# First attention of a two-layer kernel: scores with the keys as weights, the row maxima carried as two extra rows of the contraction

## What is computed

```
qh = layernorm_per_head((layernorm(x) @ Wq.T + bq))  * 16 ** -0.5      # 16 heads of 16
kh = layernorm_per_head(ctx @ Wk.T + bk);  vh = ctx @ Wv.T + bv
attn = softmax(einsum('bhqd,bhkd->bhqk', qh, kh), axis=-1)
x1 = x + einsum('bhqk,bhkd->bhqd', attn, vh).reshape(...) @ Wp.T + bp
router_logits = layernorm(x1) @ moe_router      # top 2 of 8 experts follow
```

## Time and profile before

| | us |
|---|---|
| median of 3 runs | 1415.62 |
| the profiled execution | 1416.21 |
| its span (first to last instruction) | 1414.3 |
| `qkv_phase` | 0 to 110.3 |
| `attention0_phase` | 110.5 to 371.0 |
| busy, whole span: PE, DVE, POOL, ACT | 1286.1, 918.5, 715.3, 657.7 |
| mean granted TensorE clock, of full speed | 0.95 |

### The profile page before, as it was taken

One profiled execution on the slowest core, in us unless ns is written; L12 is line 12 of the kernel. 1 busy time (PEld: TensorE's weight loads), 2 busy tenths in 40 slices (PEclk: granted clock), 3 DMA queues, 4 the chain that ended last, 5 costly groups with the idle time before them and its releaser, 6 DMA issues. The chain is left out here.

```text
span 1414.3 us, 29515 instructions
## 1 busy us (share of the span) xinstructions
PE 1286.1 (91%) x7733; PEld 1026.7 (73%) x7734; DVE 918.5 (65%) x2179; ACT 657.7 (47%) x1386; POOL 715.3 (51%) x903
## 2 busy tenths in 40 slices
PE   7997999999779999999998599857999999859998
PEld 4665777777448888888886477525888888747786
DVE  4784888888656777777776688692333333346665
ACT  2464777777325454544544477454333333221120
POOL 1223566565214655565554466306555555167775
PEclk9998999999799999999999699858999999979999
DMA  3118322222624555555554787535555556664443
GB/s 98 53 37 311 112 86 90 89 82 97 243 101 129 158 157 165 167 156 158 168 163 115 253 234 229 193 149 201 164 162 159 162 162 147 144 212 131 131 132 117
DMA packets 125980, 212.73 MB, mean 150 GB/s; under 512 B 17802, under 2 KB 92571, under 8 KB 122588
## 3 DMA queue, kind: packets, MB, share of 16 engines
q1 hardware_dynamic: 94276, 137.52, 31.5%
q0 software_dynamic: 20640, 56.39, 14.5%
q10 hardware_dynamic: 11000, 18.06, 3.4%
HBM read 148.03 MB, written 59.64 MB: 147 GB/s over the span
## 5 line engine op out<-in xcount | busy, mean ns | idle before, releaser
L1222 POOL DMA_INDIRECT xg<-t_xn,token x160 | 151.7, 948 | 154.6 <-PE psum L2120 70.6
L2196 POOL DMA_INDIRECT su_yg<-t_y,slot x128 | 122.8, 959 | 70.1 <-issue 38.1
L2132 PE MATMUL psum<-gu,m_xT 128*128 x640 | 153.0, 382 | 0.0
L2091 DVE TENSOR_TENSOR m_h<-psum,m_sg 128x256 f32<-128x256 f32 x80 | 33.9, 424 | 157.8 <-ACT m_sg L2070 157.8
L2132 PEld LDWEIGHTS psum<-gu,m_xT 128*128 128x128 f32 x640 | 116.6, 192 | 12.8
L1475 PE MATMUL psum<-w,m_xT_high 128*128 x284 | 119.0, 419 | 0.0
L1497 PE MATMUL psum<-m_both,m_hT_high 128*128 128x512 f32 x284 | 112.5, 418 | 1.4 <-DVE top_i L1441 1.3
L1475 PE MATMUL psum<-w_low,m_xT_high 128*128 x284 | 112.8, 397 | 0.0
L1475 PE MATMUL psum<-w,m_xT_low 128*128 x284 | 112.6, 397 | 0.0
L1348 POOL DMA_INDIRECT t_y<-top_v,dest x36 | 67.8, 1883 | 70.1 <-DVE top_v L1441 69.8
L1422 DVE TENSOR_TENSOR m_both<-w,m_both 128x1024 fp32r<-128x1024 f32 x71 | 87.0, 1225 | 14.1 <-ACT m_both L1390 10.9
(11 more groups left out here) (309 smaller groups left out, 3467.3 us busy)
## 6 DMA issues: line engine op xcount, KB each, us to landing
w<-in_w SPq DMA_DIRECT2D x71, 512.0 KB, 3.8
t_y<-m_y SPq DMA_DIRECT2D x80, 256.0 KB, 2.2
w<-in_w SPq DMA_DIRECT2D x8, 1024.0 KB, 11.3
t_x<-at_x SPq DMA_DIRECT2D x64, 128.0 KB, 2.0
t_w_low<-at_low ACTq DMA_DIRECT2D x64, 128.0 KB, 1.7
w_low<-t_w_low SPq DMA_DIRECT2D x8, 1024.0 KB, 13.3
at_yg<-t_y SPq DMA_DIRECT2D x32, 256.0 KB, 3.3
gu<-in_gu ACTq DMA_DIRECT2D x8, 1024.0 KB, 12.4
```

Of the source, the lines that this page charges most:

```text
L1222: pool.indirect_dma_start(out=g.xg1[j % GB][:, k * D:(k + 1) * D], out_offset=None, in_=g.xn4, in_offset=bass.IndirectOffsetOnAxis(ap=g.to ...
L2132: last = pe.matmul(ps_gu[p][:, k * 2 * M1:(k + 1) * 2 * M1], xT[p][:, at:at + P], g.gu[:, bass.ds(ex[k] * (DC * 2 * M1) + c * 2 * M1, 2 * ...
L2196: pool.indirect_dma_start(out=yg[p][k][:, :], out_offset=None, in_=g.y1, in_offset=bass.IndirectOffsetOnAxis(ap=g.slot[:, at:at + 1], axis ...
```

## The change

Queries and keys no longer stay in SBUF as they are made. In `qkv_phase` ACT writes `affine` twice (exact and rounded), POOL subtracts (`part`), and SP stores high and low to DRAM (`store`: 2 transfers for a piece of keys, 8 for a piece of queries). SP loads them back by batch (`load_queries_keys`, 9 transfers) into stacks of 96 rows, three parts of 32 (two heads of 16): `q3` = [high, high, low] and `k3` = [high, low, high], with the two heads of a pair block-diagonal in `k3` (zeros from POOL). A ring of four slots holds four batches; the first four are loaded within `qkv_phase`.

In the attention a unit is, first, half the tokens and half the heads of a batch:

1. PE makes the scores by token with four `fp32r` matmuls of 154 columns (L886 of the new kernel). They serve only the maxima, which DVE takes as before.
2. Once in two units PE transposes the maxima (L910), ACT copies them out as `mT`, and SP moves them with two transfers into rows 96 and 97 of `q3`; the same rows of `k3` hold -1 for the head's own keys.
3. Five units later PE makes four scores with the keys as weights, 98 rows deep and 256 tokens wide (L900): they come out by key with the maximum subtracted already. ACT takes exp straight from PSUM into `prT`, and PE multiplies with the values, 256 columns at a time (L965).

So DVE's subtraction, ACT's exp in SBUF, PE's 8 transposes, ACT's copy and POOL's copies for the unit go. The input norm of the router moves from DVE to ACT, the writing back of high from ACT to POOL, the store of low from ACT's queue to SP's; the top-8 results are collected for 8 tiles before they are copied; one expert's `w13` is loaded every 8 units, and the 12 loads for later phases are issued at unit 12. The lags grow (the last stage lags 20 units where it lagged 10).

```diff
 class HeadNorm:
     def affine(self, act, i, s_passed):
-        act.activation(out[:, bass.ds(i.n * n, n)], self.ps_t[:, 0:n], ACT.Identity, ...)
+        wait(act, self.s_low, i.shift(-1).n)
+        wait(act, self.st[p], i.div(2).n * self.landed)
+        for out in (self.full, self.high):
+            last = act.activation(out[p], self.ps_t[:, 0:n], ACT.Identity, bias=self.beta, scale=self.gamma)
+    def part(self, pool, i):
+        pool.tensor_tensor(self.low[p], self.full[p], self.high[p], ALU.subtract).then_inc(self.s_low, 1)
+    def store(self, sp, i):
+        for which, (rows, s_made) in enumerate(((self.high[p], self.s_out), (self.low[p], self.s_low))):
+            sp.wait_ge(s_made, i.n + 1)
+            for first, last in self.store_rows:
+                sp.dma_start(self.stored[which](i.n, first, last), ...).then_inc(self.st[p], 16)
+def load_queries_keys(sp, g, b, slot):
+    for j, part in enumerate((0, 0, 1)):
+        sp.dma_start(g.q3[slot][32 * j:32 * j + 32, :]..., g.q_parts[part][:, b, :, :]).then_inc(landed, 16)
+    for j, part in enumerate((0, 1, 0)):
+        for a in range(2):
+            sp.dma_start(g.k3[slot][at:at + DH, :]..., g.k_parts[part]...).then_inc(landed, 16)
 def qkv_phase
         def _(sp):
+            def step(s):
+                load_x(i)
+                if (at := piece(s, OUT + 1)) is not None:
+                    at[0].store(sp, at[1])
+                if s.off in PRELOAD:
+                    sp.wait_ge(q.st[b % 2], (b // 2 + 1) * q.landed)
+                    load_queries_keys(sp, g, b, b)
 def attention0_phase
-        T_RAW, T_N, T_O, T_WP, T_X, T_R = 4, 5, 6, 7, 9, 10
+        T_ST, T_PV = 5, 6
+        T_RAW, T_N, T_O, T_WP, T_INV, T_AP, T_X, T_R = 10, 12, 14, 15, 16, 17, 19, 20
         def _(sp):
+                    for a in range(2):
+                        sp.dma_start(g.q3[...][96 + a:97 + a, ...], mT[gr][96 + a:96 + HG:2, :]...).then_inc(s_mr[gr], 16)
         def _(pool):
-                    pool.tensor_copy(q_s[p][:, :], g.qT_all[:, bass.ds(t.n * D, D)]).then_inc(q_ready, 1)
-                            pool.tensor_tensor(kblk[bp_]..., ALU.mult).then_inc(k_ready, 1)
+                    pool.tensor_copy(chunk(i).bitcast(F32R), high[i.mod(2)][:, :]).then_inc(w_back, 1)
         def _(dve):
-                    dve.tensor_tensor(pr[p]..., s3, mx[p]..., ALU.subtract).then_inc(sub_done, 1)
-                    ln.apply(dve, x1[p][:, :], xn[p][:, :], t).then_inc(x_norm, 1)
         def _(act):
-                    act.activation(prT[p][0:LK, :]..., ps_tp[0:LK, :, :], ACT.Copy).then_inc(tp_out, 1)
-                    act.activation(pr[p][:, :], pr[p][:, :], ACT.Exp).then_inc(exp_done, 1)
+                    act.activation(prT[p][0:LK, :]..., ps_st[0:LK, :, :], ACT.Exp).then_inc(exp_done, 1)
+                    ln.apply_scalar(act, x1[p][:, :], xn[p][:, :], t).then_inc(x_norm, 1)
+                    act.activation(mT[gr][96:96 + HG, :], ps_m, ACT.Copy).then_inc(mt_out, 1)
         def _(pe):
+                    wait(pe, mx_ready, u.n)
+                    for i in range(HG // 2):
+                        last = pe.matmul(ps_s[...], g.q3[slot][0:96, ...128 tokens], g.k3[slot][0:96, ...2 * LK], ...)
+                    if quad % 2 == 0:
+                        pe.wait_ge(s_mr[quad // 2], (b.n + 1) * 32)
+                    wait(pe, exp_done, v.n)
+                    for j in range(QUAD):
+                        last = pe.matmul(ps_st[0:LK, ...SQ], g.k3[slot][0:98, ...LK], g.q3[slot][0:98, ...SQ], ...)
```

More of the change, by code:

```diff
@@ L174, in __init__ @@
         self.eps, self.ps_p, self.ps_t = eps, ps_p, ps_t
+        n = 2 * DC * rows
+        at = [parts[:, i * n:(i + 1) * n] for i in range(6)]
+        self.full, self.high, self.low = at[0:2], *([a.bitcast(F32R) for a in at[i:i + 2]] for i in (2, 4))
+        self.stored, self.store_rows = stored, store_rows
+        self.landed = 2 * len(store_rows) * 16
         self.sq, self.n = ([sb(f"{name}_{n}{i}", [P, 2 * D]) for i in range(2)] for n in ("sq", "n"))
@@ new lines, in store @@
+    def store(self, sp, i):
+        p = i.mod(2)
+        for which, (rows, s_made) in enumerate(((self.high[p], self.s_out), (self.low[p], self.s_low))):
+            sp.wait_ge(s_made, i.n + 1)
+            for first, last in self.store_rows:
+                sp.dma_start(self.stored[which](i.n, first, last),
+                             rows[first:last, :].bitcast(F32).rearrange("p (c t) -> p c t", c=DC)).then_inc(self.st[p], 16)
+QK_LOADS, QK_RING = 9, 4
+Q_ROWS = [(i * 2 * DH, (i + 1) * 2 * DH) for i in range(P // (2 * DH))]
@@ L329, in _, with step @@
             pool.memset(g.v_all[:, :], 1.0).then_inc(s_v1, 1)
[L331 to L337, removed]
+            for slot in range(QK_RING):
+                pool.memset(g.k3[slot][0:96, :].bitcast(F32), 0.0).then_inc(s_zero, 1)
+            def step(s):
+                if (i := pair(s, X)) is not None:
+                    p = i.mod(2)
+                    wait_alone(pool, ln_mv, i.n + 1, passed[1])
+                    inverse_root(pool, rstd[p][:, :], mv[p][:, :].rearrange("p (a n) -> p a n", a=2)[:, :, 1],
+                                 g.minus_half[:, 0:2], ln_eps, ln_rstd, i)
+                if (at := piece(s, OUT)) is not None:
+                    at[0].part(pool, at[1])
+            steps(pool, FIRST, LAST, TOTAL, BODY, step)
         @block.vector
@@ L404, in _ @@
                 act.dma_start(batches(ctxT[:, :], a, b), batches(g.ins["ctx"], a, b)).then_inc(s_landed, 16)
+            act.wait_ge(s_neg, 16)
+            for slot in range(QK_RING):
+                act.activation(g.k3[slot][96:98, :], neg[96:98, :], ACT.Copy)
             act.wait_ge(s_gs, 1)
@@ L607, in _ @@
+            few(TOTAL, half)
             for p in range(2):
@@ L714, in half @@
                 i = chunk_at(u, T_HIGH)
                 if i is not None:
-                    if i.loop is None and i.off == 0:
-                        act.wait_ge(s_w13_first, 16)
-                    if i.loop is None and i.off == CHUNKS // E0 - 1:
-                        act.wait_ge(s_w13, (E0 - 1) * 16)
-                    wait(act, low_st[i.mod(4)], i.div(4).n * 16)
-                    act.activation(low[i.mod(4)][:, :], chunk(i), ACT.Copy).then_inc(w_high, 1)
-                v = u.shift(-1)
@@ L808, in half @@
[L808 to L815 removed]
+                    last.then_inc(m_t, 1)
                 t = tile_at(u, T_O)
@@ L839, in half @@
                     pe.wait_ge(x_out, t.n + 1)
+                    wait(pe, lg_done, t.n)
                     for c in range(DC):
```

445 lines of the change are left out of this document (258 added, 187 removed).

## The result

| | before | after |
|---|---|---|
| median of the runs (lowest to highest), us | 1416.08 (1414.25 to 1416.89) | 1440.62 (1436.91 to 1444.26) |
| ratio, 95% interval | | 1.0175 [1.0141, 1.0209] |
| profiled execution, its span, us | 1416.21, 1414.3 | 1436.91, 1435.1 |
| first scores by token to the end of the attention, us | | 151.0 to 396.7 |

The account below looks back on a forecast made before the run. PE was taken to bound the attention and the query stage; 1416.2 less 42.5 in the attention, plus 34.5 for SP's issues in the query stage, less 0.6, gave 1408 us; own range 1395 to 1422, wide range 1382 to 1447.

Parts of the forecast that it names:

- PE's unit: Attention: PE's work per unit falls from 3.69 to 3.0 us, with the other engines hidden under it.
- the end: Attention's tail after the last scores: 34 us, up from 25.3, as exp and values trail four units more.
- the first rival: Scores by token: the 154-column products run at float32 pace, 1.12 us for four, giving 1443 us; chance 0.25.
- DVE's share: Attention: DVE falls to some 60% busy, 1.8 us of work a unit.
- the query stage as SP's: Query stage: 171 SP issues at 0.47 us take 80.4 us, so the attention starts 34.5 us later, at 144.9.
- The first five units: Attention's start: five units with scores by token alone, 2.0 us each, 10 us, after 1 to start.
- The second rival: Query stage: SP's issues cost their lone price, 0.33 us, so it gives back 12 us, 1386 us; chance 0.15.
- The attention's length: Whole attention: falls from 260.5 to 218 us, 42.5 less.
- It has three units, 9 us, ... of which issue and landing take some 3: Attention: the maxima's rows have 9 us from ACT's copy to PE's use and need some 3.
- plus 5 for the 12 loads: Attention, unit 12: twelve loads issued in one go ahead of the maxima's transfers add 5 us.
- The third rival: Attention: short key packets make the maxima's rows late once a batch, 24 us in all, 1432 us; chance 0.15.
- 59 units at 3.0 = 177; less 9: Attention: 59 units take 177 us, less 9 as tile products have not all begun in the next 15 units.

Follow-up runs that it names:

- run 6: The changed kernel plus one useless 512-column float32 product after the scores of each of the attention's first eight units; 1438.16 us, ratio 1.0172 to before.
- run 10: The changed kernel with 128-row-outermost query stores, experts 3 to 7 loaded in key steps, twelve loads from unit 50, first eight units filled; 1396.40 us, ratio 0.9875.
- run 4: The changed kernel with the twelve loads at unit 12 spread, one in every two units, the largest in four pieces; 1450.34 us, ratio 1.0248 to before.
- run 3: The changed kernel with the maxima's rows sent by ACT's DMA queue instead of SP's; 1437.68 us, ratio 1.0163 to before.

## Why the prediction was wrong

*Right:* PE's unit, 3.0 us; the end, 37.7 us with the last unit for 37; the narrow scores at the `fp32r` pace, so that the first rival (0.25) is out; DVE's share (85.67 of 146 us, 59%); the query stage as SP's, with 0.47 us an issue (0.49 with the gaps): 84.1 us from 66.4 for 80.4 from 64.5, and 6 late. The first five units are right by luck: 10.2 us for 11, but reckoned at the full clock and run at half. The second rival (lone price, 0.15) is out.

*Where it failed:* "The attention's length", 218 us for 245.7. Two of its steps carry the 27 us.

- "It has three units, 9 us, ... of which issue and landing take some 3", and "plus 5 for the 12 loads": this wait was mis-sized in each of its terms. The room is 7.3 us, not three whole units. The landing time came from a stretch with a DMA share of 0.33; behind the load of an expert the rows took some 5 us from issue to PE, on top of 2.6 to 4.0 in the queue, and at the twelve loads (2.7 MB, with an expert's 1 MB behind them) 7.6 on top of 8.1, with the engines full (1.07). I worked with the mean load of a batch, 10.2 of 12 us, and the mean came out near that (0.75 of the 13.0 us that a batch took, 9.7), so short packets were no dearer than reckoned; but the mean says nothing of a burst. The third rival had the mechanism, rows behind a burst of loads, and a price near it (24 us), but once in every batch and from short packets; what is shown is one stop in two batches, from bulk. Moving the bulk took 1.3% off.
- "59 units at 3.0 = 177; less 9", and the five first units: a sum at a clock of 1.00 throughout. I had the earlier trace rows with 0.80 in the end stretch and gave the clock no term. The first units, which wait for each other's maximum, ran at 0.50, and it stayed there for 38 us from the first scores on; four of the six stops lowered it again. The filled units of run 6 and the windows of run 10 show it.

Together these are larger than the 8.0 us by which the sum came out faster, so the sign turned. The time lay outside the forecast's own 1395 to 1422; that it lay in the wide range, to 1447, is luck, since that end stood for the first rival, which did not come. What remains open: why the clock stays at 0.50 in the change's first units for 28 us and more while PE is busy 99% (27.62 of 27.80), where before it was back within some 12 us of the attention's start (0.50 from 120 to 122 us, 0.98 from 122 to 124 in the profile before); which stops lower it; and the 4.9 us by which the later phases are shorter, which I did not look into.

## What to carry to other kernels

When a change turns an engine hand-over into a transfer on the path, price that transfer in the worst burst that stands ahead of it in its queue and shares the DMA engines with it, not at the mean share; count its room from one row to the other, not in whole units; and move the bulk to a stage that has room. A queue of its own brings the small transfer in time, but it costs the engine that issues it, or moves the loss to other transfers. Give the TensorE clock a term of its own: look in the profile for each place where the new order leaves PE gaps, and count the units behind the gap at half speed as well as the gap. A merged transfer must keep a large outermost dimension.

## What was not expected of the hardware

- A 256 KB store with four groups outermost ran on 4 engines (share 0.26, ACT's wait for it 57.8 us in all); with 128 rows outermost the same bytes filled 0.96 of all 16 together with the loads.
- A wait of 2.3 us cost some 8 (run 4): after it PE's products took 1.1 us instead of 0.65 for most of 14 us. A wait of 2.0 us in run 10 left the clock at 1.00.
- One useless 512-column product in each of eight units brought the clock back at least 24 us sooner (run 6).
- The two issues of the maxima's rows held ACT for 1.21 us (run 3), and SP for as long (1.21, in the change), where SP's other issues took 0.47 each in a row and 0.33 alone.
